# Clamped decay differences of a Mamba-2 block on VectorE instead of GpSimd, one head an instruction

## Chip, core and metric

The kernel runs on one core of a Trainium2 chip. The metric is device time in microseconds (us), the median of three runs of one compiled program. Lower is better.

## What is computed

A block with a Mamba-2 part and a feed-forward part over four sequences ("batches") of 512 tokens by 512 features, in fp32:

```
xn  = layernorm(x)
out = x + (xn + mamba2(xn)) + ffn(xn)
ffn(x)    = fwht(silu(x W1^T) * (x W3^T)) W2^T          (hidden width 2048)
mamba2(x) : z, xBC, dt = x w_in                          (inner width 1024, state 128, 16 heads of 64)
            xBC = silu(causal_conv4(xBC) + conv_b);  dt = softplus(dt + dt_bias);  A = -exp(A_log)
            y   = ssd(xh * dt, dt * A, B, C) + xh * D
            y   = rmsnorm(y * silu(z)) * norm_w ;  out = y w_out
```

Inside `ssd` the tokens are cut into chunks. With cs the running sum of dt * A inside a chunk, each head has a decay matrix L[l, s] = exp(cs[l] - cs[s]) for s <= l and 0 elsewhere. The kernel makes it as exp(min(cs[l] - cs[s], 0)) times a triangle that is already folded into the product of B and C.

## The kernel before

All arrays lie with 128 partitions. A batch's 50 weight tiles (10 "C" for the convolved columns, 8 "Z" for the gate, 16 "A" and 16 "U" for the two feed-forward factors) are multiplied one after another by TensorE. A tile is twelve matmuls of 128x512 (`project` and `three`, line 554: a high and a low fp16 part of each factor). Results lie in the three banks 0 to 2 in turn (the first two tiles of a batch in banks 4 and 5), so tile n waits until VectorE has evicted tile n-3. ScalarE makes a tanh or the first tap of a tile, VectorE finishes it: line 1147 three times and line 1129 once for a C tile, line 1158 for Z, 1163 for A, 1168 for U. After a U tile ScalarE copies the product to fp16 (line 899) and GpSimd takes the remainder (line 1313).

The order of all engines is one list, `make_schedule`: the tiles in order with the steps of the four 128-token chunks (c = 0 to 3) put in front of given tiles by `STEP_AT` (batches 1 to 3) and `STEP_FIRST` and `FIRST` (batch 0). Every engine walks the whole list and does its own part of each item, in order. The places are counts of A and U tiles. In batches 1 to 3 they are, for example, T at 3, 7, 17, 26; E at 6, 14, 22 for c = 1 to 3; Y at 6, 14, 22, 32; N at 8, 16, 24, 34. E of chunk 0 comes right behind the second C tile of the batch (behind the last C tile in batch 0). At the same place E stands in front of Y. The steps are these:

- T: TensorE transposes the chunk (lines 696 to 699); VectorE makes Xdt (1225); GpSimd makes XD (1336) and Xdec (1340). For c > 0 TensorE first waits for `diag_read` of chunk c-1, which is line 1251.
- E: ScalarE's queue issues a broadcast load of the chunk's cs rows, 1 MB in SBUF, into `csbc` (line 965), and for c > 0 two loads for `ecsb`. GpSimd waits for it and for TensorE's Y of the chunk before, subtracts the per-partition cs for 16 heads at once into `Eb` (1328), does a one-column marker (1331) and clamps `Eb` (1332).
- X: ScalarE exponentiates `Eb` (981), VectorE multiplies it with the triangle product (1234).
- S and R: the states of the scan (TensorE 710 and 716, VectorE 1239 and 1244, GpSimd 1346 and 1348).
- Y: sixteen matmuls with `Eb` (724), then VectorE adds XD (1251, `diag_read`) and gates (1254), then ScalarE squares and sums (988).
- N, Q, V, W: the norm and the product with w_out. N on TensorE (735) waits for ScalarE's square of Y, line 988.

After the tiles come the sixteen G steps, the product with W2 (line 759). In batch 0 the weights are also scaled and split into fp16 parts (ScalarE 847, VectorE 1098), and W2 is transformed (F: TensorE 667, ScalarE 938; H: TensorE 679, VectorE 1212).

## Time and profile before

| | |
|---|---|
| median of 3 runs | 1006.52 us (1001.41 to 1006.76) |
| the profiled execution, its own time | 1008.38 us |
| its span, first to last instruction | 1006.6 us |
| TensorE busy | 941.3 us (94%) |
| VectorE busy | 619.2 us (62%) |
| ScalarE busy | 352.7 us (35%) |
| GpSimd busy | 296.1 us (29%) |
| granted TensorE clock, mean | 0.98 of full speed |

Busy time is the sum over instructions of an engine; matmuls overlap each other, so a busy TensorE is not one at its peak. In the lists below "idle before" is time in which an engine waited in front of an instruction, with what ended the wait. Times in lists are us from the start of the span.

### The profile page before, as it was taken

How to read it: one execution, taken by the hardware profiler on the slowest of the kernel's cores; microseconds unless marked ns; L12 is line 12 of the kernel's file. 1: busy time of each engine (PE TensorE's matmuls, PEld its weight loads, DVE VectorE, ACT ScalarE, POOL GpSimd, SP SyncE). 2: the span in 40 equal slices, each digit the busy share in tenths (PEclk: the TensorE clock that was granted, in tenths of full speed). 3: DMA queues.
4: the chain of work that ended last, by engine and by line, in shares of the span. 5: the costliest groups of instructions: out<-in, count | busy, mean ns of one | idle time of the engine just before them, and what ended most of it. 6: DMA issues, size and time to landing. Idle time of an engine off the chain costs nothing.

```text
span 1006.6 us, 13195 instructions
## 1 busy us (share of the span) xinstructions
PE 941.3 (94%) x4960; PEld 469.3 (47%) x4960; DVE 619.2 (62%) x1063; ACT 352.7 (35%) x537; POOL 296.1 (29%) x180
## 2 busy tenths in 40 slices
PE   3798868999899999999999999999999999999997
PEld 2343333455344444555545445554545445555543
DVE  5776477879543566757862566767751766766621
ACT  5574744443423343331221334332221343232200
POOL 0332241536000111555500202654500202755300
PEclk9899897999899999999999999999999999999999
DMA  9589553746332434553432434554422534355123
GB/s 326 215 303 335 168 178 107 228 129 231 113 117 92 160 96 111 181 137 99 130 84 64 160 95 125 158 147 117 123 63 64 171 96 148 82 157 145 45 74 94
DMA packets 80815, 142.64 MB, mean 142 GB/s; under 512 B 8048, under 2 KB 20976, under 8 KB 78704
## 3 DMA queue, kind: packets, MB, share of 16 engines
q1 hardware_dynamic: 61536, 113.79, 36.5%
q10 hardware_dynamic: 19216, 28.01, 9.6%
q8 instruction: 40, 0.66, 0.3%
q14 instruction: 23, 0.19, 0.1%
HBM read 115.82 MB, written 25.95 MB: 141 GB/s over the span
## 4 chain that ended last, share of the span: by engine, by line
PE 75%; DVE 11%; issue 4%; ACT 4%; DMA 3%; POOL 2%; ACTq 0%; SPq 0%; DVEq 0%; POOLq 0%
PE ps L554 48%; PE ps L759 16%; DVE arena L1147 2%; PE ps L724 2%; DVE arena L1098 2%; DMA arena<-cs_rows 2%; PE ps L716 2%; PE ps L710 1%; PE ps L679 1%; PE ps L696 1%; POOL arena L1340 1%; DVE arena L1168 1%; DVE arena L1129 1%; DMA w_mid<-arena 1%; ACT arena L820 1%
## 5 line engine op out<-in xcount | busy, mean ns | idle before, releaser
L554 PE MATMUL ps<-xh,arena 128*128 128x512 f16 x1600 | 500.7, 386 | 35.5 <-DVE arena L1163 8.8
L554 PE MATMUL ps<-xl,arena 128*128 128x512 f16 x800 | 308.6, 386 | 0.0
L554 PEld LDWEIGHTS ps<-xh,arena 128*128 128x128 f16 x1600 | 160.8, 101 | 233.3 <-issue 34.2
L759 PE MATMUL ps<-arena 128*128 128x512 f16 x768 | 171.2, 379 | 0.0
L1313 POOL TENSOR_TENSOR arena<-arena 128x512 f16<-128x512 f32 x64 | 82.8, 1297 | 280.6 <-ACT arena L899 280.6
L1328 POOL TENSOR_TENSOR arena<-arena 128x2048 f32<-128x2048 f32 x16 | 57.8, 3612 | 291.6 <-DMA arena<-cs_rows 291.6
L1147 DVE SCALAR_TENSOR_TENSOR arena<-ps,cw,arena 128x511 f32<-128x511 f32 (+2 forms) x120 | 89.6, 749 | 52.5 <-ACT arena L889 50.7
L554 PEld LDWEIGHTS ps<-xl,arena 128*128 128x128 f16 x800 | 79.3, 99 | 90.8 <-issue 7.7
L759 PEld LDWEIGHTS ps<-arena 128*128 128x128 f16 x768 | 74.5, 98 | 91.2 <-issue 5.7
L899 ACT ACTIVATE arena<-arena 128x512 f16<-128x512 f32 x64 | 40.3, 630 | 211.0 <-DVE arena L1168 211.0
L554 PE MATMUL ps<-wo_hi,arena 128*128 128x512 f16 x256 | 78.8, 379 | 0.6 <-DVE arena L1276 0.6
L1098 DVE SCALAR_TENSOR_TENSOR arena<-arena,scl 128x512 f16<-128x512 f32 x50 | 53.3, 1070 | 37.9 <-ACT arena L847 37.8
L1163 DVE SCALAR_TENSOR_TENSOR arena<-arena,ps 128x512 f32<-128x512 f32 x64 | 43.8, 684 | 47.4 <-ACT arena L894 47.4
L894 ACT ACTIVATE arena<-ps,f 128x512 f32<-128x512 f32 x64 | 43.5, 679 | 76.6 <-PE ps L554 76.6
L1168 DVE SCALAR_TENSOR_TENSOR arena<-ps,arena 128x512 f32<-128x512 f32 x64 | 44.1, 690 | 23.2 <-PE ps L554 22.2
L1234 DVE TENSOR_TENSOR arena<-arena 128x2048 f32<-128x2048 f32 x16 | 42.1, 2631 | 21.4 <-ACT arena L981 21.4
L1302 DVE SCALAR_TENSOR_TENSOR arena<-ps,f_w,arena 128x512 f32<-128x512 f32 x16 | 10.9, 746 | 61.5 <-PE ps L759 61.5
L554 PE MATMUL ps<-wo_lo,arena 128*128 128x512 f16 x128 | 48.5, 379 | 0.0
L889 ACT ACTIVATE arena<-ps,cb,cw 128x512 f32<-128x512 f32 x40 | 30.9, 773 | 31.3 <-PE ps L554 26.8
L554 PEld LDWEIGHTS ps<-wo_hi,arena 128*128 128x128 f16 x256 | 25.1, 98 | 32.4 <-issue 1.8
L904 ACT ACTIVATE arena<-arena 128x512 f32<-128x512 f32 x40 | 25.2, 630 | 38.6 <-DVE arena L1147 23.5
L847 ACT ACTIVATE arena<-arena,scl 128x512 f16<-128x512 f32 x50 | 35.3, 712 | 6.0 <-DVEq L1190 3.6
(158 smaller groups left out, 1074.2 us busy)
## 6 DMA issues: line engine op xcount, KB each, us to landing
arena<-w_parts SPq DMA_DIRECT2D x198, 256.0 KB, 2.7
w_parts<-arena SPq DMA_DIRECT2D x66, 256.0 KB, 3.4
arena<-cs_rows ACTq DMA_DIRECT2D x16, 1024.0 KB, 6.1
arena<-w SPq DMA_DIRECT2D x8, 1024.0 KB, 8.5
arena<-w SPq DMA_DIRECT2D x32, 256.0 KB, 4.0
arena<-ecs_rows ACTq DMA_DIRECT2D x24, 256.0 KB, 7.7
arena<-w SPq DMA_DIRECT2D x8, 512.0 KB, 6.0
w_mid<-arena SPq DMA_DIRECT2D x16, 256.0 KB, 2.2
```

The costliest lines, as they stand in the source:

```text
L554: ins = nc.tensor.matmul(out_ap, lhs(i, a), rhs(i, c), start=(i == 0 and s == 0), stop=(i == n - 1 and s == 2))
L759: ins = nc.tensor.matmul(bank(t), hw[a][:, i, t * P:(t + 1) * P], w2s[i % W2R][:, d, :], start=(i == 0 and s == 0), stop=(i == JF - 1 and ...
L847: nc.scalar.activation(part_hi[p % PARTS], raw_tile(p), ACT.Copy, scale=scl[:, n:n + 1]).then_inc(w_hi.sem, 1)
L894: nc.scalar.activation(slot, src, ACT.Tanh, scale=(f_half if kind == "Z" else f_13)[:, 0:1]).then_inc(tanh_ok.sem, 1)
L899: nc.scalar.activation(hid_hi[:, i, :], hs[i % 2], ACT.Copy).then_inc(hid_h.sem, 1)
L1098: nc.vector.scalar_tensor_tensor(out=part_lo[p % PARTS], in0=raw_tile(p), scalar=scl[:, n:n + 1], in1=part_hi[p % PARTS], op0=ALU.mult, op ...
L1147: ins = nc.vector.scalar_tensor_tensor(out=a[:, s:L], in0=src[:, 0:L - s], scalar=cw[:, i, TAPS - 1 - s:TAPS - s], in1=a[:, s:L], op0=ALU. ...
L1163: nc.vector.scalar_tensor_tensor(out=hs[i % 2], in0=tb[tanh[key] % 2], scalar=1.0, in1=src, op0=ALU.add, op1=ALU.mult).then_inc(evac.sem, 1)
L1168: nc.vector.scalar_tensor_tensor(out=hs[i % 2], in0=src, scalar=HID / (2 * XS * XS), in1=hs[i % 2], op0=ALU.mult, op1=ALU.mult).then_inc(e ...
L1234: nc.vector.tensor_tensor(Eb, Eb, Gm.unsqueeze(1).to_broadcast([P, NH, P]), ALU.mult).then_inc(m_ok.sem, 1)
L1313: nc.gpsimd.tensor_tensor(hid_lo[:, i, :], hs[i % 2], hid_hi[:, i, :], ALU.subtract).then_inc(hid_l.sem, 1)
L1328: nc.gpsimd.tensor_tensor(Eb, csbc, cs_s[:, c * NH:(c + 1) * NH].unsqueeze(2).to_broadcast([P, NH, P]), ALU.subtract).then_inc(esub_ok.sem, 1)
```

## The change

The two GpSimd instructions of step E, and the marker between them, go. In step E VectorE waits for the same three semaphores as GpSimd did and issues sixteen `tensor_scalar` instructions, one for each head: `Eb[:, h, :] = min(csbc[:, h, :] - cs_s[:, h], 0)` with the per-partition cs as a pointer scalar. Only the last signals, and `esub_ok` is merged into `emin_ok`. The lower clamp at -3.0e38 of line 1332 goes too; in its place `dt * A` is clamped at -1.0e35 once a batch, one more VectorE instruction of 128x64 in front of the running sums. The places of all steps stay as they were.

```diff
@@ signals
-        esub_ok = signal("esub_ok", NC, 1)
-        emin_ok = signal("emin_ok", NC)
+        emin_ok = signal("emin_ok", NC, 1)
@@ SyncE, kind HL
-                        sp.wait_ge(esub_ok.sem, esub_ok.at(0, NC - 1))
+                        sp.wait_ge(emin_ok.sem, emin_ok.at(0, NC - 1))
@@ ScalarE, kind E
-                        act.wait_ge(esub_ok.sem, esub_ok.at(b, c - 1))
+                        act.wait_ge(emin_ok.sem, emin_ok.at(b, c - 1))
@@ dve_dt
-            nc.vector.tensor_tensor(heads(av), heads(dtv), nega[:].unsqueeze(1).to_broadcast([P, NC, NH]),
-                                    ALU.mult).then_inc(dt_a.sem, 1)
+            k = steps.step(nc.vector.tensor_tensor(heads(av), heads(dtv), nega[:].unsqueeze(1).to_broadcast([P, NC, NH]), ALU.mult))
+            dve.wait_ge(steps.sem, k)
+            nc.vector.tensor_scalar(av, av, -1.0e35, None, ALU.max).then_inc(dt_a.sem, 1)
@@ VectorE
+                    elif kind == "E":
+                        dve.wait_ge(d_csbc, (b * NC + (c + 1)) * 16)
+                        dve.wait_ge(sums_ok.sem, sums_ok.at(b, 0))
+                        dve.wait_ge(pe_diag.sem, pe_diag.at(b, c - 1))
+                        for h in range(NH):
+                            ins = nc.vector.tensor_scalar(Eb[:, h, :], csbc[:, h, :], cs_s[:, c * NH + h:c * NH + h + 1], 0.0,
+                                                          ALU.subtract, ALU.min)
+                        ins.then_inc(emin_ok.sem, 1)
@@ GpSimd
-                    elif kind == "E":
-                        pool.wait_ge(d_csbc, (b * NC + (c + 1)) * 16)
-                        pool.wait_ge(sums_ok.sem, sums_ok.at(b, 0))
-                        pool.wait_ge(pe_diag.sem, pe_diag.at(b, c - 1))
-
-                        nc.gpsimd.tensor_tensor(Eb, csbc, cs_s[:, c * NH:(c + 1) * NH].unsqueeze(2).to_broadcast([P, NH, P]),
-                                                ALU.subtract).then_inc(esub_ok.sem, 1)
-                        pool.wait_ge(esub_ok.sem, esub_ok.at(b, c))
-                        nc.gpsimd.tensor_tensor(pool_mark[:], ones[:, 0:1], ones[:, 0:1], ALU.mult)
-                        nc.gpsimd.tensor_scalar(Eb, Eb, 0.0, -3.0e38, ALU.min, ALU.max).then_inc(emin_ok.sem, 1)
```

VectorE in batch 1 around step E of chunk 2 (place 14), before: U tile 6 (line 1168), then Y of chunk 1 (1251, 1254).

```order
L1163 SCALAR_TENSOR_TENSOR arena<-arena,ps 128x512 [waits hid_l,tanh_ok]
L1168 SCALAR_TENSOR_TENSOR arena<-ps,arena 128x512 [waits evac,tile_done]
L1251 TENSOR_TENSOR arena<-ps,arena 128x1024 [waits t2_ok,pe_diag]
L1254 SCALAR_TENSOR_TENSOR arena<-arena,f_half 128x1024 [waits diag_read]
L1163 SCALAR_TENSOR_TENSOR arena<-arena,ps 128x512 [waits hid_l,tanh_ok]
```

The same place in the changed kernel, where lines 1251 and 1254 have become 1259 and 1262.

```order
L1163 SCALAR_TENSOR_TENSOR arena<-arena,ps 128x512 [waits hid_l,tanh_ok]
L1168 SCALAR_TENSOR_TENSOR arena<-ps,arena 128x512 [waits evac,tile_done]
L1236 TENSOR_SCALAR arena<-arena 128x128 [waits pe_diag,sums_ok,d_csbc]
L1236 TENSOR_SCALAR arena<-arena 128x128 x15
L1259 TENSOR_TENSOR arena<-ps,arena 128x1024 [waits t2_ok,pe_diag]
L1262 SCALAR_TENSOR_TENSOR arena<-arena,f_half 128x1024 [waits diag_read]
L1163 SCALAR_TENSOR_TENSOR arena<-arena,ps 128x512 [waits hid_l,tanh_ok]
```

The wait for the load (`d_csbc`) and the sixteen instructions now stand between the eviction of a tile and Y of the chunk before. TensorE's order does not change. Behind its sixteen Y matmuls (line 724) it has two tiles, and then N (735), which waits for `sq_ok`, ScalarE's square of Y; these are its rows of before, the first of each group.

```order
L724 MATMUL ps<-arena 64x128 x15
L554 MATMUL ps<-xh,arena 128x512 [waits evac,d_parts0]
...
L554 MATMUL ps<-xh,arena 128x512 [waits evac,d_parts1]
...
L735 MATMUL ps<-arena,con 128x1 [waits mamba_evac,sq_ok]
```

Nothing moved there: what is new is only what VectorE does ahead of the signal that line 735 waits for.

VectorE in batch 1 around step E of chunk 0, changed kernel: the second C tile (1147 three times, 1129), step E, the third C tile, a Z tile (1158).

```order
L1147 SCALAR_TENSOR_TENSOR arena<-ps,cw,arena 128x509 [waits dve_steps]
L1236 TENSOR_SCALAR arena<-arena 128x128 [waits pe_diag,sums_ok,d_csbc]
L1236 TENSOR_SCALAR arena<-arena 128x128 x15
L1147 SCALAR_TENSOR_TENSOR arena<-ps,cw,arena 128x511 [waits acc_ok]
L1147 SCALAR_TENSOR_TENSOR arena<-ps,cw,arena 128x510 [waits dve_steps]
L1147 SCALAR_TENSOR_TENSOR arena<-ps,cw,arena 128x509 [waits dve_steps]
L1158 SCALAR_TENSOR_TENSOR arena<-arena,ps 128x512 [waits tanh_ok]
```

Before, the two rows of line 1236 were not there, and the rows of line 1147 followed each other.

## Rows read from the trace of the kernel before

**Rows 1.** The page: span, and busy us (share) xinstructions of each engine

```profile
span 1006.6 us, 13195 instructions
...
PE 941.3 (94%) x4960; PEld 469.3 (47%) x4960; DVE 619.2 (62%) x1063; ACT 352.7 (35%) x537; POOL 296.1 (29%) x180
```

**Rows 2.** Waits of TensorE, 340 to 620 us: line, releaser, total us, times, longest

```profile
PE ps L554 <- DVE arena L1147: 3.2, 2, 1.6
PE ps L716 <- POOL arena L1340: 1.2, 1, 1.2
```

**Rows 3.** The sixteen loads into csbc (line 965), from issue to landing

```profile
DMA to landing us min/median/max: 4.7/6.1/8.9
```

**Rows 4.** Timeline, batch 1, chunks 2 and 3: start us, us, instruction [idle before]

```profile
436.22 0.33 ACTq L965 DMA_DIRECT2D arena<-cs_rows  x1
...
437.34 1.23 DVE L1251 TENSOR_TENSOR arena<-ps,arena 128x1024 f32<-128x1024 f32 x1 [1.22 <-PE ps L724]
438.60 1.28 DVE L1254 SCALAR_TENSOR_TENSOR arena<-arena,f_half 128x1024 f32<-128x1024 f32 x1
...
442.42 0.28 PE L735 MATMUL ps<-arena,con 128*128 128x1 f32 x2
...
444.70 3.61 POOL L1328 TENSOR_TENSOR arena<-arena 128x2048 f32<-128x2048 f32 x1 [6.68 <-DMA arena<-cs_rows]
...
474.25 1.06 ACT L988 ACTIVATE arena<-arena 128x1024 f32<-128x1024 f32 x1 [3.13 <-DVE arena L1254]
```

**Rows 5.** Timeline, batch 1, chunk 1 (place 6)

```profile
404.45 1.23 DVE L1251 TENSOR_TENSOR arena<-ps,arena 128x1024 f32<-128x1024 f32 x1 [1.88 <-PE ps L724]
...
406.94 1.04 PE L696 MATMUL ps<-con,arena 128*128 128x128 f32 x8
...
408.04 3.61 POOL L1328 TENSOR_TENSOR arena<-arena 128x2048 f32<-128x2048 f32 x1 [3.57 <-DMA arena<-cs_rows]
```

**Rows 6.** Front of batch 1: chain (first row), then timeline

```profile
335.53 18.25 PE ps L554 x84
...
345.52 3.76 DVE L1147 SCALAR_TENSOR_TENSOR arena<-ps,cw,arena 128x510 f32<-128x510 f32 x5
...
349.52 3.61 POOL L1328 TENSOR_TENSOR arena<-arena 128x2048 f32<-128x2048 f32 x1 [78.87 <-DMA arena<-cs_rows]
...
350.01 3.67 DVE L1129 SCALAR_TENSOR_TENSOR arena<-arena 128x512 f32<-128x512 f32 x1
...
357.98 0.38 PE L554 MATMUL ps<-xh,arena 128*128 128x512 f16 x1 [1.63 <-DVE arena L1147]
```

**Rows 7.** Timeline of VectorE: the nearest instructions with pointer scalars

```profile
12.38 1.46 DVE L1088 TENSOR_SCALAR arena<-arena 128x512 f32<-128x512 f32 x3
...
20.80 0.23 DVE L1111 TENSOR_SCALAR cw<-cw,f_half 128x8 f32<-128x8 f32 x1
20.93 0.17 DVE L1112 TENSOR_SCALAR cb<-cb 128x10 f32<-128x10 f32 x1
```

**Rows 8.** Timeline, batch 0, chunks 0, 2 and 3

```profile
88.79 0.74 DVE L1098 SCALAR_TENSOR_TENSOR arena<-arena,scl 128x512 f16<-128x512 f32 x1
...
93.46 3.61 POOL L1328 TENSOR_TENSOR arena<-arena 128x2048 f32<-128x2048 f32 x1 [16.72 <-DMA arena<-cs_rows]
...
186.13 3.61 POOL L1328 TENSOR_TENSOR arena<-arena 128x2048 f32<-128x2048 f32 x1 [5.79 <-DMA arena<-cs_rows]
...
188.86 0.28 PE L735 MATMUL ps<-arena,con 128*128 128x1 f32 x2
...
227.72 0.28 PE L735 MATMUL ps<-arena,con 128*128 128x1 f32 x2
...
229.03 3.61 POOL L1328 TENSOR_TENSOR arena<-arena 128x2048 f32<-128x2048 f32 x1 [6.00 <-DMA arena<-cs_rows]
```

**Rows 9.** Windows on TensorE: stretch, us, busy us (xmatmuls), clock, DMA, GB/s

```profile
97.80:103.20 5.40, 0.00 (x0) 0.70 0.33 121
103.30:106.60 3.30, 3.30 (x8) 0.50 0.82 255
```

More of the change, by code:

```diff
@@ L215, in build @@
         nws = sb("nws", [P, QE])
-        pool_mark, first = sb("pool_mark", [P, 1]), sb("first", [P, 1])
+        first = sb("first", [P, 1])
         f_in, f_half0, f_half, f_13, f_out, f_w2, f_had = (
```

## Prediction, made before the changed kernel was run

> **What bounds the kernel.** I read the page first, then TensorE's waits, then the timeline around every step E. TensorE is busy for 94% of the span, VectorE for 62% and GpSimd for 29% [rows 1]. TensorE waits little in batches 1 to 3: between 340 and 620 us the two kinds of wait in the list add up to 4.4 us [rows 2]. So each microsecond in which TensorE stands still is one more at the end, and VectorE's 380 idle microseconds are only of use if they lie where TensorE does not need it. The question is not how many microseconds of work VectorE gets, but what is queued behind them.
>
> Now the load that step E waits for. It takes 4.7 to 8.9 us from issue to landing, 6.1 at the median [rows 3]. For chunks 1 to 3 of batches 1 to 3 ScalarE issues it only once VectorE has evicted the U tile ahead, which is the moment at which VectorE itself comes to step E. In chunk 2 of batch 1 it is issued at 436.22 and GpSimd begins at 444.70, having been idle for 6.68 us [rows 4]. GpSimd had nothing else to do, so the wait cost nothing. VectorE meanwhile did Y of chunk 1 at 437.34 and 438.60 [rows 4]. In the changed kernel it stands in front of these until 444.70.
>
> **The new instructions.** None like them is in the trace: 128x128, fp32, one pointer scalar. The nearest are of 8 columns with one pointer, after which the next starts 0.13 us later, and three of 512 columns with two pointers in 1.46 us, or 0.49 each [rows 7]. Between these ends the slope is 0.7 ns a column, which makes 0.13 + 120 * 0.0007 = 0.21 us for 128 columns, 3.4 us for sixteen. Below, a bound is 16 * 0.13 = 2.1 us. Above it is 16 * 0.31 = 5.0 us, if they did not overlap (0.23 us is the duration of the one of 8 columns [rows 7], plus 0.08 for the columns). I take 3.4, since instructions without a wait between them do overlap in these rows. It is near what GpSimd's subtraction alone took (3.61 us, [rows 4]).
>
> The page "VectorE: DVE Perf Modes" of the Trainium skill (section on the TRN2 errata) gives 58 + columns/2 cycles for such an instruction in its double-rate mode. That would be an estimate of 2.0 us for sixteen, and the total would be 16 * 1.4 = 22 us lower. It also says there that the fixed part is paid for each instruction and that small tiles suffer, which speaks against cutting one pass into sixteen. The rows of three agree that a fixed part of 0.13 us is most of it.
>
> **Chunks 2 and 3, batches 1 to 3.** Behind Y's matmuls TensorE has two tiles and then N, which needs ScalarE's square of Y. That square needs lines 1251 (1.2 us) and 1254 (1.3), and takes 1.1 itself [rows 4]. New time of the square: landing + 3.4 + 1.2 + 1.3 + 1.1 = landing + 7.0 us. In chunk 2 of batch 1 this is 451.7, and TensorE comes to N at 442.42 [rows 4], so it stands for 9.3 us. N comes 6.2 us after the issue in each of these places; hence the loss is the load's time plus 0.8. The six loads, read like the one in the rows, took 8.5, 7.9, 4.8 (chunk 2) and 8.9, 8.3, 7.6 us (chunk 3), all inside the bounds [rows 3]. The sum is 46.0 + 4.8 = 50.8 us.
>
> **Chunk 1, batches 1 to 3.** Here T of chunk 1 comes one tile behind Y of chunk 0, and needs line 1251. TensorE is at T at 406.94; the load lands at 408.04 [rows 5], so line 1251 ends at 408.04 + 3.4 + 1.2 = 412.6: a stand of 5.7 us. The load of batch 2 is as long, that of batch 3 is 0.7 longer. Sum 17.8 us. The N behind it is then covered by the tile between.
>
> **Chunk 0, batches 1 to 3.** VectorE gets to step E at about 347.0 (345.52 and two of five instructions of 0.75), the load lands at 349.52 [rows 6]. Step E ends at 352.9 and the third C tile's three passes at 355.2. TensorE needs that bank for its seventh tile, which would start at 335.53 + 6 * 2.61 = 351.2 [rows 6]. It loses 4.0 us. But a loss goes as well: line 1129 takes 3.67 us at 350.01 where it usually takes 0.7, until GpSimd's line 1328 (349.52 to 353.13) is over, and through ScalarE this makes TensorE wait 1.63 us at 357.98 [rows 6]. With GpSimd idle that is gone. Net 2.4 us, 7.2 for three.
>
> The page "SBUF — State Buffer" of the skill (section "Who interferes with whom") says that a VectorE instruction with two SBUF inputs, or in a two-port mode, and a GpSimd instruction exclude each other for their whole length. By that rule, the trace agrees: 3.67 against 0.7 us. It is the rule that speaks most for the change, and a rival below rests on the mechanism.
>
> **The clock.** After TensorE had done nothing from 97.8 to 103.2 us the granted clock was 0.50, the lower of its two levels (1.2 and 2.4 GHz), and only 8 matmuls started in the next 3.3 us [rows 9], where at 0.217 us each (18.25 us for 84, [rows 6]) 15 would have. This costs 3.3 - 8 * 0.217 = 1.6 us. I take it for all twelve new stands of 4 to 10 us in batches 1 to 3: 19.2 us. Bounds: nothing and 19.2.
>
> **GpSimd's queue.** TensorE's wait of 1.2 us for line 1340 [rows 2] has its cause in GpSimd doing E, and XD and Xdec only behind it. That goes: minus 1.2 us.
>
> **Batch 0.** Chunk 0: VectorE is at the place at 88.79; the load lands at 93.46 [rows 8], so everything behind moves by 93.46 + 3.4 - 88.8 = 8.1 us. The W2 transform, on which TensorE then waits, starts from the silu of the last C tile behind it. Chunk 2: 186.13 + 7.0 - 188.86 = 4.3 us. Chunk 3: 229.03 + 7.0 - 227.72 = 8.3 us [rows 8]. In chunk 1 TensorE loses some 5.7 us at T like in the other batches, but VectorE's split instructions there no longer stand behind GpSimd; between 0 and 5.7 I take 2. With the clock for two stands (3.2) batch 0 gives 25.9 us.
>
> The clamp of dt * A is four instructions of 128x64; three run beside G matmuls. The one in batch 0 may add 0.2 us. Nothing for that.
>
> **Sum.** 50.8 + 17.8 + 7.2 + 19.2 - 1.2 + 25.9 = 119.7 us. The profiled execution took 1008.4 us by its own time, so the changed kernel takes 1128; the median of the three runs is 1.9 us under that execution, so I forecast 1126.
>
> **Rivals.**
> 1. The clock stays up or drops only sometimes. For: stands at other places come at other moments than the one I saw. Against: rows 9. Time: 1126 - 22 = 1104.
> 2. The sixteen instructions do not overlap, 5.0 us in place of 3.4: 16 * 1.6 = 26 us more, 1152. Against: the 0.13 us of rows 7, smaller than the duration of 0.23.
> 3. TensorE's lead covers the wait for the load, and only VectorE's own 3.4 us count: 16 * 3.4 = 54 us, 1060. This would be so if the load were issued well ahead of VectorE. Against: in chunks 1 to 3 it is issued at VectorE's own arrival, and the two tiles in front of N are 5.2 us.
> 4. The other side: lifting GpSimd's exclusion of VectorE pays, and the wait is covered. It decides if the square of Y is done when TensorE comes to N, which asks for a load of less than -0.8 us in chunks 2 and 3; at T of chunk 1 the load would have to land at 402.3, before TensorE's Y is even done; only in chunk 0 could it be reached, by a landing at 345.5. Gain in that case 3 * 1.6 + 1.2 and some 5 in batch 0, or 997 us. The skill's rule on the shared port is the one that speaks for it; the time is from the rows. The rows leave it hardly a chance.
>
> **How the numbers follow.** Forecast 0.70; rival 1 0.11; rival 2 0.10; rival 3 0.06; rival 4 0.02; within 0.5% 0.01. The range takes in rivals 1 and 2 with some room: loads all at 4.7 us would take off some 30 us, all at 8.9 would add some 35, and neither will hold for all. 1095 to 1158 us. Faster by over 0.5%: 0.02, within 0.5% (about what a measurement of this kernel can tell): 0.01, slower: 0.97.
>
> **What would show it.** Right: in the profile after, VectorE's line 1236 waits some 5 to 8 us for cs_rows at each step E and about 100 us in all; its sixteen instructions take 3 to 4 us start to end; TensorE waits for ScalarE's square at line 735 for about 9 us in six places and for line 1259 at 696 in three; the granted clock is at its lower level behind these. TensorE's busy share falls to about 85%, GpSimd's busy time by some 90 us. Line 1129 has no instruction of 3.7 us any more. Wrong: no wait at 735 (then rival 3 or 4), waits of the named size with a clock of 1.0 (rival 1), or a step E of 5 us (rival 2).

## The result, and the profile after

The changed kernel took 1122.01 us (median of four runs, 1116.38 to 1125.59), the kernel before 1004.93 us beside it (four runs, 1001.41 to 1006.76). The ratio is 1.1165, with a 95% interval of 1.1106 to 1.1223: slower by some 117 us. The forecast was 1126 us, between 1095 and 1158. The profiled execution took 1116.38 us by its own time, with a mean granted clock of 0.944 (before 0.98). It is the shortest of the four, so between the two profiled executions lie 108.0 us, and all that is read from rows below adds up to that number and not to 117.

First the page of the changed kernel, span and busy time by engine, and the clock in 40 slices. It answers to [rows 1].

```profile
span 1114.6 us, 13407 instructions
...
PE 966.9 (87%) x4960; PEld 478.3 (43%) x4960; DVE 638.7 (57%) x1323; ACT 354.1 (32%) x537; POOL 199.2 (18%) x132
...
PEclk9898989889999998988999898988999999988999
```

GpSimd lost 97 us of work (296.1 to 199.2), and VectorE got only 20 more (619.2 to 638.7): its 256 new instructions are busy for 51.6 us, and its other ones for some 32 us less than before (line 1129 alone for 8.3 us less). VectorE is busy for 57% of the span. So by busy time alone no engine is any nearer to a bound, and yet the kernel is 108 us longer by its span. The slices of the clock show eights from end to end, where before there were only nines from batch 1 on.

The waits of the changed kernel (line, releaser, total us, times, longest) name what the busy time can't.

```profile
PE ps L734 <- ACT arena L987: 52.0, 7, 9.1
PE ps L695 <- DVE arena L1259: 21.3, 4, 5.6
...
PE ps L553 <- DVE arena L1147: 12.5, 6, 3.9
...
PE ps L666 <- DVE arena L1158: 7.3, 1, 7.3
```

```profile
DVE arena L1236 <- DMA arena<-cs_rows: 87.4, 16, 8.6
```

VectorE stands in front of all sixteen steps E, 87.4 us in all. TensorE stands for what VectorE then has behind it: N (734) for ScalarE's square, T (695) for Y's first line (1259), a tile (553) for a C tile's eviction, the W2 transform of batch 0 (666) for a Z tile's (1158). Before, TensorE's whole list from 340 to 620 us held 4.4 us of waits [rows 2]. The chain that ended last says the same in shares of the span (the page's first and second line of it):

```profile
PE 60%; DVE 18%; DMA 10%; issue 6%; ACT 6%; ACTq 0%; SPq 0%; DVEq 0%
PE ps L553 38%; PE ps L758 15%; DMA arena<-cs_rows 9%; DVE arena L1236 5%; DVE arena L1147 2%; DVE arena L1098 2%; PE ps L709 1%; DVE arena L1168 1%; PE ps L695 1%; DVE arena L1259 1%; ACT arena L980 1%; PE ps L678 1%; ACT arena L819 1%; DVE arena L1262 1%; PE ps L715 1%
```

Nine per cent of the span is the load itself, five are the new instructions.

One step in full, batch 1, step E of chunk 2 (timeline: start us, us, instruction, idle before). It is the place of [rows 4].

```profile
466.45 0.33 ACTq L964 DMA_DIRECT2D arena<-cs_rows  x1
...
474.98 3.22 DVE L1236 TENSOR_SCALAR arena<-arena 128x128 f32<-128x128 f32 x16 [8.62 <-DMA arena<-cs_rows]
478.12 1.22 DVE L1259 TENSOR_TENSOR arena<-ps,arena 128x1024 f32<-128x1024 f32 x1
479.37 1.28 DVE L1262 SCALAR_TENSOR_TENSOR arena<-arena,f_half 128x1024 f32<-128x1024 f32 x1
480.69 1.06 ACT L987 ACTIVATE arena<-arena 128x1024 f32<-128x1024 f32 x1 [13.67 <-DVE arena L1262]
481.89 0.59 PE L734 MATMUL ps<-arena,con 128*128 128x1 f32 x2 [9.08 <-ACT arena L987]
```

The load is issued at 466.45, and VectorE is idle from then until it lands. The load lands at 474.95 (8.50 us after its issue). The sixteen new instructions, the two lines of Y and ScalarE's square end at 481.75, which is 6.8 us after it, and TensorE has been idle for 9.08 us.

### The profile page after: what moved, and what is told of

It is laid out like the page before. It is cut to its first block, busy times and chain, and to the rows that moved or that the text cites. A ratio compares the mean times of both kernels' runs of the same rounds, so it can differ in the third digit from the quotient of the medians.

```text
span 1114.6 us, 13407 instructions
## 1 busy us (share of the span) xinstructions
PE 966.9 (87%) x4960; PEld 478.3 (43%) x4960; DVE 638.7 (57%) x1323; ACT 354.1 (32%) x537; POOL 199.2 (18%) x132
## 4 chain that ended last, share of the span: by engine, by line
PE 60%; DVE 18%; DMA 10%; issue 6%; ACT 6%; ACTq 0%; SPq 0%; DVEq 0%
PE ps L553 38%; PE ps L758 15%; DMA arena<-cs_rows 9%; DVE arena L1236 5%; DVE arena L1147 2%; DVE arena L1098 2%; PE ps L709 1%; DVE arena L1168 1%; PE ps L695 1%; DVE arena L1259 1%; ACT arena L980 1%; PE ps L678 1%; ACT arena L819 1%; DVE arena L1262 1%; PE ps L715 1%
## 5 line engine op out<-in xcount | busy, mean ns | idle before, releaser
L553 PE MATMUL ps<-xh,arena 128*128 128x512 f16 x1600 | 513.6, 395 | 37.9 <-DVE arena L1147 12.5
L553 PE MATMUL ps<-xl,arena 128*128 128x512 f16 x800 | 315.7, 395 | 0.0
L553 PEld LDWEIGHTS ps<-xh,arena 128*128 128x128 f16 x1600 | 164.1, 103 | 244.6 <-issue 49.4
L1321 POOL TENSOR_TENSOR arena<-arena 128x512 f16<-128x512 f32 x64 | 75.6, 1181 | 742.1 <-ACT arena L898 742.1
L1236 DVE TENSOR_SCALAR arena<-arena 128x128 f32<-128x128 f32 x256 | 51.6, 280 | 87.4 <-DMA arena<-cs_rows 87.4
L1098 DVE SCALAR_TENSOR_TENSOR arena<-arena,scl 128x512 f16<-128x512 f32 x50 | 46.3, 932 | 33.2 <-ACT arena L846 33.2
L987 ACT ACTIVATE arena<-arena 128x1024 f32<-128x1024 f32 x16 | 16.9, 1057 | 145.4 <-DVE arena L1262 145.4
L734 PE MATMUL ps<-arena,con 128*128 128x1 f32 x32 | 6.9, 285 | 55.9 <-ACT arena L987 52.0
L1334 POOL TENSOR_TENSOR arena<-arena,dcol 128x1024 f32<-128x1024 f32 x16 | 37.9, 2370 | 23.8 <-DVE arena L1259 23.8
```

The source lines that it names most:

```text
L553: ins = nc.tensor.matmul(out_ap, lhs(i, a), rhs(i, c), start=(i == 0 and s == 0), stop=(i == n - 1 and s == 2))
L1098: nc.vector.scalar_tensor_tensor(out=part_lo[p % PARTS], in0=raw_tile(p), scalar=scl[:, n:n + 1], in1=part_hi[p % PARTS], op0=ALU.mult, op ...
L1236: ins = nc.vector.tensor_scalar(Eb[:, h, :], csbc[:, h, :], cs_s[:, c * NH + h:c * NH + h + 1], 0.0, ALU.subtract, ALU.min)
L1321: nc.gpsimd.tensor_tensor(hid_lo[:, i, :], hs[i % 2], hid_hi[:, i, :], ALU.subtract).then_inc(hid_l.sem, 1)
L1334: nc.gpsimd.tensor_tensor(XD.rearrange("p (q l) -> p q l", q=QE), XT[:, 0:QE, c * P:(c + 1) * P], dcol[:].unsqueeze(2).to_broadcast([P, QE ...
```

## The experiments

I worked with two theories. **A**: the time is made at the place. VectorE arrives when the load is only being issued, stands there, and then works, with Y behind it; TensorE waits for the sum of the two, and the clock drops behind each stand. **B**: the work itself is what costs (sixteen small instructions, rival 3 of the prediction), or VectorE is too loaded to take it, wherever it stands. All medians below stand against the kernel before on the same chip.

### The wait without the work

The kernel before, with GpSimd still doing the differences. VectorE only waits where the changed kernel has it wait.

```diff
+                    elif kind == "E":
+                        dve.wait_ge(d_csbc, (b * NC + (c + 1)) * 16)
+                        dve.wait_ge(pe_diag.sem, pe_diag.at(b, c - 1))
                     elif kind == "X":
```

> The kernel before, with one addition: in step E VectorE waits for the load of the cs rows and for Y of the chunk before, as in the change, but does nothing there; GpSimd makes the differences as ever. Theory (VectorE is held in front of Y by the load, then by its own sixteen instructions, and TensorE pays for both): each stand shrinks by the 3.2 us of work. Chunks 2 and 3: 50.8 - 6 * 3.2 = 32 us, chunk 1: 17.8 - 3 * 3.2 = 8 us, fronts of batches 1 to 3: 3 us, batch 0: 12 us, clock 1.6 us for some nine stands: 14 us. Total 69 us over the kernel before, 1074 us. Rival W (the work does the harm, 256 more instructions on VectorE, and the wait is hidden): within 10 us of 1005.

Measured: 1093.35 us (1089.04 to 1099.08, four runs), ratio 1.0868 (1.0816 to 1.0920). That is 87 us with not one instruction moved. It is 19 more than I expected, and the timeline at step E of chunk 2 shows where from:

```profile
467.10 3.61 POOL L1331 TENSOR_TENSOR arena<-arena 128x2048 f32<-128x2048 f32 x1 [7.02 <-DMA arena<-cs_rows]
...
468.31 3.48 DVE L1257 SCALAR_TENSOR_TENSOR arena<-arena,f_half 128x1024 f32<-128x1024 f32 x1
```

The landing now releases VectorE and GpSimd at one moment. GpSimd's subtraction (467.10 to 470.71) has begun before VectorE's gate of Y (1257, two inputs in SBUF), which takes 3.48 us in place of 1.28 and ends 1.08 us after the other's end. It is so at twelve of the sixteen gates, and the median of all is 3.48 us too:

```profile
L1257 DVE SCALAR_TENSOR_TENSOR arena<-arena,f_half x16: 1283/3476/3480, 141.3 to 1042.5; 128x1024 f32<-128x1024 f32 x16
```

So this run holds the wait and, by accident, 2.2 us more at twelve steps, 26 us in all. Most of the loss is there with no work moved, but the 87 us are not the price of the wait alone: without the 26 some 60 would be left, an estimate.

### More and less work at the same place

The sixteen instructions done twice (the second time with the same result), and one 128x2048 instruction in place of the sixteen. That one subtracts the first head's cs for all heads, so it leaves out what the step is for; it only stands for less work at the same place.

```diff
                             ins = nc.vector.tensor_scalar(Eb[:, h, :], csbc[:, h, :], cs_s[:, c * NH + h:c * NH + h + 1], 0.0,
                                                           ALU.subtract, ALU.min)
+                        dve.wait_ge(steps.sem, steps.step(ins))
+                        for h in range(NH):
+                            ins = nc.vector.tensor_scalar(Eb[:, h, :], csbc[:, h, :], cs_s[:, c * NH + h:c * NH + h + 1], 0.0,
+                                                          ALU.subtract, ALU.min)
```

> The changed kernel with the sixteen instructions of each step E done twice (a wait for the last of the first sixteen between), so VectorE holds 3.4 us longer at each of 16 places. Theory: every microsecond ahead of Y is one for TensorE, since TensorE already stands there: 16 * 3.4 = 54 us more than the change, 1176 us. Rival S (TensorE has slack left at some places, or VectorE's time there is hidden): clearly less than 54 us, say 1140 us.

```diff
-                        for h in range(NH):
-                            ins = nc.vector.tensor_scalar(Eb[:, h, :], csbc[:, h, :], cs_s[:, c * NH + h:c * NH + h + 1], 0.0,
-                                                          ALU.subtract, ALU.min)
+                        ins = nc.vector.tensor_scalar(Eb, csbc, cs_s[:, c * NH:c * NH + 1], 0.0, ALU.subtract, ALU.min)
```

> The changed kernel with one instruction of 128x2048 in place of the sixteen; it subtracts the first head's cs for all heads, so 15 heads get other differences than they should. All waits stay. It should take 1.3 us (2048 columns at 0.52 ns, as two of three passes of 512 columns show, and 0.13), which is 1.9 us less at each of 16 places. Theory (one to one, as the doubled run showed with 50 us for 16 * 3.2): 1122 - 16 * 1.9 = 1092 us. With the run of twice the work this makes a line over 1.3, 3.2 and 6.4 us of work. Rival I (what hurts is the number of instructions, a fixed price for each of 256, or their pointer scalars): the same 1092, but then the run with two large instructions is below the change as well.

Measured: twice 1171.50 us (1168.24 to 1176.88), ratio 1.1646 (1.1598 to 1.1694); once in one 1081.52 us (1076.62 to 1084.07), ratio 1.0755 (1.0719 to 1.0790). The rows of the two, the first a timeline row of the doubled kernel, the second all sixteen of the other (ns min/median/max):

```profile
491.36 3.22 DVE L1236 TENSOR_SCALAR arena<-arena 128x128 f32<-128x128 f32 x16 [5.67 <-DMA arena<-cs_rows]
494.62 3.22 DVE L1240 TENSOR_SCALAR arena<-arena 128x128 f32<-128x128 f32 x16
```

```profile
L1235 DVE TENSOR_SCALAR arena<-arena x16: 1285/1286/1287, 93.5 to 984.2; 128x2048 f32<-128x2048 f32 x16
```

Work of 1.3, 3.2 and 6.5 us a step gives 1081.5, 1122.0 and 1171.5 us. Over sixteen steps that is 1.3 us at the end for each us of work between the first two, and 0.95 between the last two. So each us of work behind the landing is about one us of the kernel's time: nothing hides it. Drawn on to no work, with a slope between 0.95 and 1.3, the line comes to 1055 to 1062 us. That is an estimate: some 49 to 56 us for the wait, 60 to 67 for the work (what each brings with it in the clock is in these numbers). Theory A holds both, and the wait without the work (B's price of it is nothing) is not small.

### Two full-width instructions

Subtraction with a broadcast operand and then the minimum, each 128x2048, on VectorE.

```diff
+                        k = steps.step(nc.vector.tensor_tensor(Eb, csbc, cs_s[:, c * NH:(c + 1) * NH].unsqueeze(2).to_broadcast([P, NH, P]),
+                                                               ALU.subtract))
+                        dve.wait_ge(steps.sem, k)
+                        ins = nc.vector.tensor_scalar(Eb, Eb, 0.0, None, ALU.min)
```

> The changed kernel with two instructions of 128x2048 in place of the sixteen: GpSimd's subtraction with a broadcast operand, now on VectorE (2.3 us, as line 1234 of this size takes when nothing holds it), and a clamp at 0 (1.3 us). In all 3.6 us in place of 3.2, full result. Theory: 16 * 0.4 = 6 us more, 1128 us. Rival I (cutting one pass into sixteen small instructions is what costs, as the skill's advice on small tiles says): below 1110 us.

Measured: 1126.82 us (1122.37 to 1130.74), ratio 1.1205 (1.1162 to 1.1248). The groups by line:

```profile
L1235 DVE TENSOR_TENSOR arena<-arena 128x2048 f32<-128x2048 f32 x16 | 36.7, 2293 | 89.8 <-DMA arena<-cs_rows 89.8
...
L1238 DVE TENSOR_SCALAR arena<-arena 128x2048 f32<-128x2048 f32 x16 | 19.6, 1227 | 0.5
```

2.29 + 1.23 = 3.5 us against 3.2. By the slope the 0.3 us should cost some 5; it cost 4.8, though the two intervals overlap. Two large instructions or sixteen small ones make no clear difference as long as they take the same time.

### The work at another place

The changed kernel, with only VectorE's part of step E moved, into a step D of its own. ScalarE still issues the load at step E. For chunks 1 to 3, D comes at places 9, 16 and 25 (of the count of A and U tiles), for chunk 0 of batches 1 to 3 some tiles later in the front, in batch 0 behind F1.

```diff
@@ STEP_AT (in STEP_FIRST the same)
+    "D": (None, 9, 16, 25),
@@ batch front
                 seq.append(("E", 0))
+            if len(seq) == 9:
+                seq.append(("D", 0))
@@ VectorE
-                    elif kind == "E":
+                    elif kind == "D":
                         dve.wait_ge(d_csbc, (b * NC + (c + 1)) * 16)
```

> The changed kernel, but VectorE's part of step E comes later in the order, when the load has landed: chunk 1 behind tile 8 of A and U (place 9), chunk 2 at 16 behind N and its reduction, chunk 3 at 25, chunk 0 later in the front (batch 0: after two F steps). The load stays where it is. All 256 instructions are still done by VectorE. Theory: no stand is left, VectorE's 3.2 us lie beside TensorE's tiles, GpSimd no longer blocks VectorE or delays Xdec: 995 to 1005 us, a little faster than the kernel before. Rival W (the work does the harm): above 1050 us.

Measured: 1008.24 us (1007.36 to 1010.01, ten runs), ratio 1.0020 (0.9997 to 1.0042). 114 of the 117 us are gone, with the same instructions on the same engine. The page:

```profile
span 1005.6 us, 13407 instructions
...
PE 941.3 (94%) x4960; PEld 468.5 (47%) x4960; DVE 637.6 (63%) x1323; ACT 352.7 (35%) x537; POOL 199.0 (20%) x132
```

VectorE is as busy as in the changed kernel (637.6 against 638.7 us), TensorE as before (941.3). Its list of waits has no `cs_rows` but one of 1.1 us. That refutes B as told: VectorE has room for the work, for all sixteen instructions a step. I had expected a small gain, since GpSimd's differences can no longer hold VectorE; there is none to measure.

### Chunk 0 alone left at its place

The same kernel, with only chunk 0's part back where the change put it (in batch 0 too, directly behind E).

```diff
@@ against the kernel with the work moved
                 seq.append(("E", 0))
-            if len(seq) == 9:
-                seq.append(("D", 0))
+                seq.append(("D", 0))
```

> The kernel of e3 (VectorE's part late), with chunk 0 alone left where the change has it: right behind the load in the front of each batch, right behind the last C tile in batch 0. Theory, by the sum of the prediction: 8.1 us in batch 0 and 2.4 + 1.6 us in each other batch, 20 us over e3, 1028 us. Rival (the front has slack): within 5 us of e3's 1008.

Measured: 1027.44 us (1026.49 to 1028.83, four runs), ratio 1.0208 (1.0157 to 1.0258). The sum came as expected, but not its parts. By the starts of the batches, chunk 0 costs 5.5, 5.6 and 5.4 us in batches 1 to 3. I had written 4.0 each, with GpSimd's hold given back; but that is gone from the kernel this one stands against as well, and the prediction's terms without it, 4.0 and 1.6 for the clock, are 5.6. In batch 0 it costs only 4.4, where the prediction had 8.1. VectorE's waits for the load of chunk 0, one in each batch:

```profile
DVE arena L1238 <- DMA arena<-cs_rows: 11.1, 4, 4.6
```

### The load issued earlier

Now the other half: ScalarE issues the load at an earlier place (a step L: the head of a batch, then places 2, 10 and 18), and VectorE's part stays in front of Y.

```diff
@@ STEP_AT (in STEP_FIRST 4 in place of 2)
+    "L": (None, 2, 10, 18),
@@ ScalarE
-                    elif kind == "E":
+                    elif kind == "L":
...
                                       cs_rows[b, c].rearrange("h l -> (h l)").partition_broadcast(P)).then_inc(d_csbc, 16)
+                    elif kind == "E":
```

> The changed kernel, but ScalarE issues the cs load three to four tiles earlier (at places 2 or 4, 10, 18, and at the head of a batch for chunk 0; in batch 0 chunk 0 it stays), VectorE's part stays in front of Y. Theory: the wait for the load is gone, the 3.2 us of work are still ahead of Y, of which TensorE's slack covers 1.2 us: (3.2 - 1.2) * 9 = 18 us in batches 1 to 3 and about 15 us in batch 0, less some 8 us for what GpSimd no longer does; no drop of the clock, as these stands are short: 1005 + 25 = 1030 us. Rival W (work): as slow as the change, 1122 us.

Measured: 1048.43 us (1044.80 to 1049.69, four runs), ratio 1.0414 (1.0369 to 1.0459). The wait for the load is gone but for one place, and 74 us with it. 42 stay, where I had expected about 24. Timeline, step E of chunk 2:

```profile
446.86 3.60 DVE L1239 TENSOR_SCALAR arena<-arena 128x128 f32<-128x128 f32 x16 [1.32 <-PE ps L725]
...
454.15 0.38 PE L736 MATMUL ps<-arena,con 128*128 128x1 f32 x2 [2.15 <-ACT arena L990]
```

Two things I had left out. `Eb` is free only when TensorE's Y of the chunk before is done, and that is the very moment at which VectorE's own lines of Y could start. So the work can't use the idle time in front of it, and lies on the path whole. (Here it takes 3.60 us and not 3.22: GpSimd's line 1324, from 446.29 to 447.45, holds the first of the sixteen, which have one tensor input in SBUF each. The longest such step is 5.19 us.) And I had expected no drop of the clock behind such short stands. There are eight in batches 1 to 3, one of them behind this stand of 1.96 us:

```profile
414.65 1.24 PE L697 MATMUL ps<-con,arena 128*128 128x128 f32 x8 [1.96 <-DVE arena L1262]
```

```profile
415.40:418.80 3.40, 3.40 (x12) 0.50 0.24 77
...
sum 27.30, PE 26.89; mean PE 3.36
```

The sum is over windows on all eight: TensorE is busy for 26.9 us at half the clock. At the full clock that work would take half as long, so some 13 of the 42 us are the clock's.

### The same load, with GpSimd

The kernel before, with the same early load; GpSimd's and VectorE's code is not touched.

```diff
@@ STEP_AT of the kernel before
+    "L": (None, 2, 10, 18),
@@ ScalarE
-                    elif kind == "E":
+                    elif kind == "L":
...
+                    elif kind == "E":
                         if c > 0:
```

> The kernel before, GpSimd doing step E, with only the load issued as early as in e4 and e8. It tells whether e8 owes its lead to the early load or to GpSimd's work being gone. Theory (the early load alone is worth nothing, as GpSimd's wait cost nothing; worse, its subtraction now starts right behind Y's matmuls and holds VectorE's gating instruction, line 1254, which has two SBUF operands, for some 2.3 us, of which 1.2 are slack): about 9 * 1.1 = 10 us over the kernel before, 1016 us. Rival (the early load is what makes e8 fast): 1002 us.

Measured: 1023.27 us (1017.64 to 1025.38, six runs), ratio 1.0160 (1.0120 to 1.0199). An earlier load makes the kernel before slower. Timeline, and the gate of Y over all sixteen:

```profile
442.91 3.61 POOL L1331 TENSOR_TENSOR arena<-arena 128x2048 f32<-128x2048 f32 x1
443.52 4.08 DVE L1257 SCALAR_TENSOR_TENSOR arena<-arena,f_half 128x1024 f32<-128x1024 f32 x1
```

```profile
L1257 DVE SCALAR_TENSOR_TENSOR arena<-arena,f_half x16: 1285/3570/4640, 138.6 to 972.4; 128x1024 f32<-128x1024 f32 x16
```

GpSimd now starts when Y's matmuls end, just ahead of VectorE's gate, and makes it 2.3 us longer at the median. In the kernel before, that gate began at 438.60 and GpSimd at 444.70 [rows 4], some 5 us behind its end. Its lateness kept the two engines apart. At this place GpSimd's version costs 17 us and VectorE's 42. That fits what the rows show (GpSimd holds one of Y's two instructions for 2.3 us, VectorE's own 3.2 to 3.6 us stand ahead of both), though the two sums were not followed to the end.

### Load early, work behind Y

What both halves together ask for: the load as early as in the two above, and VectorE's part directly behind Y (places 6, 14, 22), chunk 0 as in the kernel with the work moved.

```diff
@@ STEP_AT
+    "L": (None, 2, 10, 18),
...
     "Y": (6, 14, 22, 32),
+    "D": (None, 6, 14, 22),
```

> The load early as in e4, and VectorE's part of step E right behind its part of Y (line 1262) instead of in front; chunk 0 as in e3. VectorE then waits there for ScalarE's tanh anyway (1.8 us), so 1.4 of the 3.2 us delay an eviction, which TensorE's two tiles of lead cover. Theory: no stand left, GpSimd does not hold VectorE or Xdec back: 998 to 1005 us, level with or just under the kernel before. Rival: another wait ends last in its place (the mean on VectorE behind it, or the ecsb loads), 1010 us or more.

Measured: 1001.85 us (1000.06 to 1004.15, twelve runs), ratio 0.9968 (0.9949 to 0.9987). It is the fastest of all, 0.3% below the kernel before, with an interval that excludes one. The gain is small. Of the 5.7 us between the two profiled spans 5.1 are there when batch 1 begins (331.55 against 336.62), where several of TensorE's old waits in batch 0 are about a microsecond shorter. In batches 1 to 3 the three waits of 1.6 us that GpSimd's hold had made are gone, and three of 0.7 to 0.9 stand a few tiles behind.

### The clock, twice

The prediction has 19.2 us for the clock. To test it, TensorE must be kept busy during a stand that stays as long as it is. The first try puts 24 matmuls whose result is not used into a spare bank in front of N, for two of the stands of each of batches 1 to 3.

```diff
                     elif kind == "N":
+                        if b > 0 and c in (1, 2):
+                            pe.wait_ge(mamba_evac.sem, mamba_evac.at(b, c - 1))
+                            for _ in range(24):
+                                nc.tensor.matmul(bank(FREE_BANK), wo_hi[:, 0, 0:P], wo_hi[:, 1, :], start=True, stop=True)
```

> The changed kernel with 24 matmuls of 128x512 more (5.2 us, results thrown away in a free bank) in front of TensorE's wait for the square of Y, for chunks 1 and 2 of batches 1 to 3. They lie inside the stands, which the profile of the change has at 5.8 to 9.1 us. Theory (a stand also costs a stretch at the lower clock behind it, 1.6 us each): the clock stays at its upper level at these six places, 6 * 1.6 = 10 us less, 1112 us. Rival C (the lower clock costs nothing, as other engines set the pace behind a stand): 1122 us, or a little more where a stand is shorter than the added work.

Measured: 1117.60 us (1108.28 to 1122.77, four runs), ratio 1.1109 (1.1059 to 1.1159), whose interval overlaps that of the changed kernel. It hardly tested what it was for. The timeline of one of the six places and the window behind (stretch, us, then by engine busy us and count, clock, DMA share, GB/s):

```profile
482.71 0.59 PE L738 MATMUL ps<-arena,con 128*128 128x1 f32 x2 [3.30 <-ACT arena L991]
```

```profile
482.70:486.00 3.30, 3.29 (x9) 1.46 (x10) 2.59 (x5) 1.17 (x2) 0.51 (x1) 0.50 0.00 0
```

The matmuls ended 3.3 us ahead of the square, and the clock behind was still 0.50. It fell at four of the six places. In the profiled execution (at 1119.77 us a slow one of the four) TensorE is busy at 0.50 for 45.8 us in batches 1 to 3, no less than in the changed kernel (below). The second try adds nine more once VectorE's first line of Y is done, and 24 in front of T too: nine stands in all.

```diff
@@ in front of T
+                            if b > 0 and c == 1:
+                                pe.wait_ge(ffn_evac.sem, ffn_evac.at(b, FREE_BANK - NC))
+                                fill(24)
                             pe.wait_ge(diag_read.sem, diag_read.at(b, c - 1))
@@ in front of N
+                        if b > 0 and c in (1, 2):
+                            pe.wait_ge(mamba_evac.sem, mamba_evac.at(b, c - 1))
+                            fill(24)
+                            pe.wait_ge(diag_read.sem, diag_read.at(b, c))
+                            fill(9)
                         pe.wait_ge(sq_ok.sem, sq_ok.at(b, c))
```

> The changed kernel with matmuls of 128x512 (results thrown away) that fill more of each stand: 24 in front of T of chunk 1, and for chunks 1 and 2 24 in front of N, then a wait for line 1259, then 9 more, all in batches 1 to 3. The first such run left 3.3 us of each stand empty behind its 24, and the clock behind it was 0.50 as before, so it did not test the question. Theory: now the clock stays at its upper level behind nine stands: 9 * 1.6 = 14 us less than the change, 1108 us, and windows behind the stands with a clock of 1.0. Rival C (the lower clock costs nothing): clock 1.0 behind them and the time of the change, 1122 us.

Measured: 1104.60 us (1100.55 to 1111.52, six runs), ratio 1.0976 (1.0930 to 1.1021), 17.4 us under the changed kernel. The same place, and the clock's line of the page:

```profile
476.42 2.12 PE L627 MATMUL ps<-wo_hi 128*128 128x512 f16 x9 [0.58 <-DVE arena L1271]
478.91 0.38 PE L746 MATMUL ps<-arena,con 128*128 128x1 f32 x2 [0.38 <-ACT arena L999]
```

```profile
PEclk9898989889999999999999999999999899999999
```

The matmuls took nothing off VectorE's waits, which are even longer (96.1 us against 87.4); what differs is the clock behind them. The windows behind the stand above, and over all stretches at 0.50 in batches 1 to 3, of which this kernel has four (the last row is their sum):

```profile
478.90:482.30 3.40, 3.11 (x15) 1.00 0.00 0
```

```profile
sum 17.10, PE 15.50; mean PE 3.88
```

The same sum over the changed kernel's eleven stretches:

```profile
sum 75.10, PE 45.81; mean PE 4.16
```

TensorE is busy at half the clock for 30.3 us less, and half of that, 15.2 us, is what the clock gives back. The medians say 17.4, with 9 to 29 between the two intervals. The profiled executions are only 5.2 us apart in batches 1 to 3, but there this kernel waits 8.5 us longer for loads; 13.7 in all. Over nine stands these are 1.5 to 1.9 us each, where 1.6 was foretold. That it is not nothing is shown.

## Why the prediction was right

It said 1126 us, and 1122 came, for the reasons given. The nearness is partly luck: for the profiled execution the sum was 119.7 us and 108.0 came. Of these 11.7 us too many, 7.2 are in batch 0, 6.3 of them in one wrong step, and 4.5 in batches 1 to 3. These 4.5 are two errors that partly cancel: 8.9 us too many for the stands, as the loads and the work were shorter, and 4.4 too few for the clock. By its steps:

**Who waits for what.** Line 1236 was to wait 5 to 8 us at each step and 100 in all: it waits 2.1 to 8.6, 87.4 in all. In chunks 1 to 3 of batches 1 to 3 it is 5.2 to 8.6, as foretold (the loads took 5.0 to 8.5 us in this run); chunk 0 of those batches waits only 2.1 to 2.4, which its own term had right and the general sentence had not. TensorE was to wait at 734 in six places and at 695 in three: it does (44.5 and 15.9 us in batches 1 to 3).

**The sixteen instructions: 3.4 us.** They took 3.22, 0.20 us from start to start. The slope drawn between two far rows [rows 7] held. The estimate from the page "VectorE: DVE Perf Modes" of the Trainium skill (section on the TRN2 errata) was 2.0 us; the measurement decides against it here. The same section says that its row comes out too short for single instructions and that the measured fixed part is about 150 cycles and not 58. With that the estimate is 0.22 us for one, 3.6 for sixteen, much nearer to the 3.22. Rival 2, no overlap, would have shown 16 * 0.28 = 4.5 us, and did not.

**Chunks 2 and 3: 50.8 us.** The six stands at N are 9.08, 7.18, 7.90, 6.29, 5.83 and 8.24 us, 44.5 in all. The rule "load's time plus 0.8" gives 9.3 for the first of them from a load of 8.5, and 8.5 was what this one took; the others came shorter with their loads and with the 0.2 us saved on the work.

**Chunk 1: 17.8 us.** Stands of 5.15, 5.18 and 5.60 us, 15.9 in all. Timeline, the last of them:

```profile
941.64 1.94 PE L695 MATMUL ps<-con,arena 128*128 128x128 f32 x8 [5.60 <-DVE arena L1259]
```

**Chunk 0: 4.0 us lost, 1.63 given back.** Stands of 3.82, 3.88 and 3.59 us at line 553, and nowhere 1.63 beside them. The give-back is in the rows of line 1129 (ns min/median/max), 3693 at most before. The stand of batch 1, and that line:

```profile
373.68 0.38 PE L553 MATMUL ps<-xh,arena 128*128 128x512 f16 x1 [3.82 <-DVE arena L1147]
```

```profile
L1129 DVE SCALAR_TENSOR_TENSOR arena<-arena x40: 679/682/1358, 30.6 to 921.4; 128x512 f32<-128x512 f32 x40
```

The page "SBUF — State Buffer" of the Trainium skill (section "Who interferes with whom") has the rule behind it, that these two engines exclude each other for a whole instruction. The waits-only kernel and the early load with GpSimd agree with it: 1.28 us became 3.5 to 4.6.

**The clock: 19.2 us.** The filled stands bear it out (1.5 to 1.9 us each over nine, and more than nothing by both intervals). Rival 1, a clock that stays up, is refuted. But the term was too small, and its upper bound as well. By the sum above TensorE is busy for 45.8 us at half the clock in batches 1 to 3, which costs 22.9; before, the clock was 1.00 all through them. The prediction took 1.6 us from one place for all twelve. Behind the longest stand, 9.08 us, TensorE was busy for 5.5 us at the lower clock, which costs 2.7; behind one of the twelve, the 3.59 us in batch 3, the clock did not fall. The window of [rows 9] has its like behind the stand at 481.89, then come the one without a drop and batches 1 to 3 of before (all TensorE: stretch, us, busy us, clock, DMA share, GB/s):

```profile
481.90:485.30 3.40, 3.40 (x10) 0.50 0.00 0
...
881.50:884.90 3.40, 3.34 (x16) 1.00 0.00 0
```

```profile
336.60:1004.00 667.40, 658.14 (x3560) 1.00 0.41 116
```

**Batches 1 to 3 in all.** The batches start, by the first copy of each, at these times (before, then after):

```profile
336.62 0.16 DVE L1171 COPY arena<-arena 128x4 f32<-128x4 f32 x1
```

```profile
355.31 0.16 DVE L1171 COPY arena<-arena 128x4 f32<-128x4 f32 x1
```

From there to the end of the span it is 670.0 us before and 759.3 after: 89.3 more, and the steps had 93.8. Of the 89.3, the stands make 44.5 + 15.9 + 11.3 = 71.7; old waits are gone, three of some 1.6 us and one of 1.2 [rows 2], 6.0 together. What is left is 89.3 - 71.7 + 6.0 = 23.6 us, and the clock's 22.9 are all of it but 0.7.

**The step that failed: batch 0, 25.9 us.** It was 18.7. "Everything behind moves by 8.1 us" in chunk 0 is the term that was too large. VectorE's arrival and the landing were read rightly, and TensorE does stand at the W2 transform for 7.31 us; what was not asked is what the delay replaces. In the kernel before, TensorE stood there too, one tile later, for ScalarE's copy of the transform (line 938; the idle stretch of [rows 9] is this one), and behind the new stand that old one is gone. This is read from the rows; no run tried it by itself. The old stand (before) and the new one (after):

```profile
103.28 0.59 PE L554 MATMUL ps<-xh,arena 128*128 128x512 f16 x1 [5.50 <-ACT arena L938]
```

```profile
97.36 5.18 PE L666 MATMUL ps<-arena,hads 128*128 128x512 f32 x6 [7.31 <-DVE arena L1158]
```

Ahead of that copy ScalarE squares the next W2 tiles, and for this it waits until the transformed ones are written out of a buffer. The write took 7.3 us from its issue at 94.04 before, and 2.0 us from 101.19 after, so the wait is shorter when everything comes later:

```profile
101.36 1.06 ACT L820 ACTIVATE arena<-arena 128x1024 bf16<-128x1024 f32 x1 [6.86 <-DMA w_mid<-arena]
```

```profile
103.23 1.06 ACT L819 ACTIVATE arena<-arena 128x1024 bf16<-128x1024 f32 x1 [1.58 <-DMA w_mid<-arena]
```

6.86 us of wait before (the first row) and 1.58 after (the second): of some 7 us of delay only 1.9 arrive at this instruction. The two kernels start the same matmuls in the same order, so the delay can be read from one matmul to the next. It is 1.8 us when TensorE comes to T of chunk 1, where the prediction had 8.1. (Chunk 0 alone at its place cost 4.4, but against a kernel that was itself 1.8 us ahead of the kernel before at that T, by shorter waits of its own; against the kernel before it is 1.3 there.)

In chunk 1 TensorE stands for 5.40 us at T, and two old waits behind it shrink: 2.00 us to nothing, and 5.93 to 3.44. T after, and these waits before:

```profile
144.13 1.94 PE L695 MATMUL ps<-con,arena 128*128 128x128 f32 x8 [5.40 <-DVE arena L1259]
```

```profile
142.86 0.38 PE L554 MATMUL ps<-xh,arena 128*128 128x512 f16 x1 [2.00 <-DVE arena L1168]
...
152.40 0.59 PE L554 MATMUL ps<-xh,arena 128*128 128x512 f16 x1 [5.93 <-DVE arena L1163]
```

It comes to 2.4 us, where the prediction took 2. A wait for line 1168 behind it is 1.2 us longer than before (4.12 against 2.93); nobody foretold that, and its cause was not looked for. Chunks 2 and 3 stand for 3.97 and 7.46 us, near their terms of 4.3 and 8.3. With the clock, and with old waits behind them that are shorter, they come to 5.2 and 8.1 us, 13.3 where the terms and 3.2 for the clock make 15.8. So 18.7 = 1.8 + 2.4 + 1.2 + 5.2 + 8.1. The same question, what the delay replaces, answers for both of the terms that were too large.

**Rivals 3 and 4.** Rival 3 held that only the work counts, 1060 us. The work did cost some 60 to 67 us by the line above, more than the 54 it said, but the wait for the load came on top. Rival 4, that GpSimd's hold was worth more than the wait, fell at the start; though its mechanism is real, and costs 2.2 us or more a step as soon as GpSimd starts at another moment, the kernel before had it in places where 6.0 us of TensorE's waits hang on it in batches 1 to 3. Removing it at no other cost (the work moved) gained nothing that can be measured.

**What changed the size of the loss.** The change put 52 us of work on an engine that idles for 380, and lost 117. 114 of them went away when the work was moved by two or three tiles (five in the front of a batch). The old places did no harm on GpSimd, which could stand idle in front of a load; on an engine that others wait for they do.

## What to carry to other kernels

Before work is moved to another in-order engine, read at its place when its inputs arrive and what is queued behind it on the new engine; a wait that was free on an idle engine is paid by everything behind it, load and work together. If the data isn't there yet when the engine comes, move the work behind what is ready, or issue the load a few tiles earlier, and look which buffer then becomes the last release. For a delay near the start of a kernel, look for a wait of another kind that it shortens, before it is counted in full.

## What the runs showed of the hardware

- TensorE's granted clock was back at 0.50 behind an idle stretch of 3.3 us, although 24 matmuls stood right before it. With no idle stretch over 0.6 us in the same place it stayed at 1.0. The length of a stand did not tell by itself: the clock fell just behind one of 1.96 us and stayed up behind one of 3.59.
- The eleven drops of the changed kernel in batches 1 to 3 cost 22.9 us (half of the 45.8 in which TensorE was busy at 0.50), 2.1 each and 1.6 to 2.7 by the single windows. Stands filled with matmuls gave back 1.5 to 1.9 each.
- A VectorE instruction with two inputs in SBUF took 3.5 to 4.6 us in place of 1.28 when a GpSimd subtraction of 3.61 us had started ahead of it. A `tensor_scalar` of 128x128 with one tensor input in SBUF was held too, 0.66 us in place of 0.28, by a GpSimd instruction of 1.16 us. Which instruction is held depends on when a load lands, and issuing a load earlier made the kernel before 1.6% slower.
- Sixteen `tensor_scalar` of 128x128 fp32 with a pointer scalar took 3.22 us (0.28 each, 0.20 from start to start). One of 128x2048 took 1.29 us: cut by head, the same columns cost 2.5 times as much.
